# Transposes of the probabilities moved around the scores, and V's matmuls moved ahead of the subtraction of the maxima

## The reference, cut to what matters

```python
x = x + self_attention(layernorm(x))           # 16 heads of 8, a query sees the 32 keys up to itself
x = x + cross_attention(layernorm(x), ctx)     # 16 heads of 8, a window of 16 keys, with biases
x = x + experts(layernorm(x))                  # top 2 of 8, hidden width 512
# each attention: softmax(mask(q @ k.T * scale)) @ v, then @ w_out
```

## Time and profile before

| | us |
|---|---|
| median of 3 runs | 622.54 (619.52 to 624.52) |
| the profiled execution, its own time | 620.3 |
| its span from first to last instruction | 617.9 |
| TensorE busy | 507.6 (82% of the span) |
| VectorE busy | 386.4 (63%) |
| ScalarE busy | 335.4 (54%) |
| GpSimd busy | 311.0 (50%) |

### The profile page before, as it was taken

How to read it: one execution, slowest core, us unless ns; L and a number is a source line. 1 busy time by engine, 2 the same in 40 slices (tenths; PEclk the granted TensorE clock), 3 DMA queues, 4 the chain that set the end, 5 groups by cost and what they waited for, 6 DMA issues and landing times.

```text
span 617.9 us, 30506 instructions
## 1 busy us (share of the span) xinstructions
PE 507.6 (82%) x11885; PEld 413.1 (67%) x11885; DVE 386.4 (63%) x1314; ACT 335.4 (54%) x981; POOL 311.0 (50%) x417
## 2 busy tenths in 40 slices
PE   1769999999988988879788888886179999999940
PEld 1446777777765665657576666655069999999940
DVE  4537788888864567666666666654526666665626
ACT  1547677777776776666666666653223444333410
POOL 3524445444453446655555555654605555545533
PEclk9979999999999999998989899986559999999985
DMA  7160000000000001100000001000222222222229
GB/s 225 54 275 30 22 27 27 28 25 25 27 22 12 16 13 30 34 29 26 26 26 26 26 27 30 28 30 19 76 49 71 70 66 68 70 65 61 56 94 328
DMA packets 36481, 34.92 MB, mean 57 GB/s; under 512 B 5934, under 2 KB 32688, under 8 KB 36161
## 3 DMA queue, kind: packets, MB, share of 16 engines
q1 hardware_dynamic: 20144, 15.42, 7.9%
q10 hardware_dynamic: 11952, 10.07, 5.8%
q0 software_dynamic: 4320, 8.53, 4.1%
HBM read 18.58 MB, written 11.68 MB: 49 GB/s over the span
## 4 chain that ended last, share of the span: by engine, by line
PE 58%; issue 14%; another core or an unknown queue 13%; DVE 4%; DMA 3%; ACT 3%; SPq 2%; ACTq 1%; POOL 1%; DVEq 0%; POOLq 0%
PE p_scores L1006 9%; PE p_probsT L523 7%; PE p_att_bank L513 6%; PE p_scores L408 5%; PE p_att_bank L1015 5%; PE p_v_bank L1015 5%; PE p_scores L453 3%; PE p_scores L401 2%; PE p_v_bank L478 2%; PE p_att_bank L463 2%; PE p_qk L420 2%; PE p_v_bank L494 2%; DVE x L312 1%; PE p_scores L1021 1%
## 5 line engine op out<-in xcount | busy, mean ns | idle before, releaser
L643 POOL TENSOR_TENSOR k_heads<-qk,consts 128x512 f32<-128x512 f32 x64 | 66.7, 1042 | 121.0 <-ACT qk L573 65.7
L1091 POOL DMA_INDIRECT expert_results<-weighted,result_at x71 | 74.7, 1053 | 77.0 <-DVE weighted L1079 41.4
L718 DVE TENSOR_REDUCE shift<-p_scores 128x8 bf16<-128x512 f32 x128 | 82.4, 686 | 34.1 <-PE p_scores L408 33.9
L550 ACT COPY probsT<-p_probsT 128x512 f32<-128x512 f32 x128 | 75.6, 591 | 26.1 <-PE p_probsT L523 24.5
L513 PE MATMUL p_att_bank<-values,probsT 128*32 128x36 f32 x4096 | 66.6, 205 | 24.9 <-issue 24.9
L1055 ACT ACTIVATE hidden<-p_scores 128x512 f32<-128x512 f32 x71 | 42.4, 598 | 77.2 <-PE p_scores L1006 52.2
L523 PE MATMUL p_probsT<-consts,probs 128*128 128x128 f32 x512 | 83.1, 287 | 0.5 <-ACT probsT L550 0.2
L513 PEld LDWEIGHTS p_att_bank<-values,probsT 128*32 128x32 f32 x4096 | 53.3, 111 | 39.6 <-issue 32.9
L556 ACT ACTIVATE probs<-p_scores 128x512 f32<-128x512 f32 x128 | 77.9, 609 | 0.1
L1006 PE MATMUL p_scores<-gotT,w_now 128*128 128x128 f32 x568 | 77.8, 281 | 0.0
L855 POOL DMA_INDIRECT sent_rows<-row,slot_u x64 | 64.3, 1004 | 15.8 <-issue 15.5
(11 more groups left out here) (131 smaller groups left out, 962.6 us busy)
## 6 DMA issues: line engine op xcount, KB each, us to landing
got<-sent_rows ACTq DMA_DIRECT2D x71, 66.0 KB, 1.9
swapped<-raw SPq DMA_DIRECT2D x64, 64.0 KB, 1.9
w<-w_in ACTq DMA_DIRECT2D x2, 2048.0 KB, 11.9
back<-expert_results SPq DMA_DIRECT2D x8, 512.0 KB, 6.8
ctxT<-ctxT_in SPq DMA_DIRECT2D x32, 64.0 KB, 1.9
out<-x SPq DMA_DIRECT2D x8, 256.0 KB, 5.0
x<-x_in SPq DMA_DIRECT2D x4, 448.0 KB, 10.1
expert_results<-weighted,result_at POOLq DMA_INDIRECT x71
```

The costliest lines, as they stand in the source:

```text
L550: nc.scalar.copy(probsT[:, 4 * half:4 * half + 4, :], p_probsT[:, :].rearrange("p (m q) -> p m q", q=P)).then_inc(s_pT, 1)
L643: nc.gpsimd.tensor_tensor(k_heads[:, :, BLK:], qk[:, 1:2, :].to_broadcast([P, G, P]), cv(C_HEAD, G).unsqueeze(2).to_broadcast([P, G, P]), ...
L718: nc.vector.tensor_reduce(shift[:, half * 8:half * 8 + 8], p_scores[:, half * 8:half * 8 + 8, 0:WIN], AX.X, ALU.max).then_inc(s_max, 1)
L1091: nc.gpsimd.indirect_dma_start(out=results, out_offset=bass.IndirectOffsetOnAxis(ap=result_at[:, slot:slot + 1], axis=0), in_=weighted[:, ...
```

## The change

On TensorE `turn_probs(0)` moves to the head of the step, in front of the scores; it waits for the first half of the exponentials alone. `turn_probs(1)` moves right behind the scores. V's matmuls move from behind it to a place between the transpose of the attention output and the subtraction; the transposes of x stay where they were. On ScalarE both copies of the transposed probabilities move to the head of the step, in front of the copies of `p_qk`, and in self-attention the copy to `raw` moves behind both exponentials. No instruction but one wait is added or taken away (V's matmuls of the cross-attention now wait for `s_x3T` themselves).

```diff
 def pe_step(h, c):
+                if runs(h, c, 0):
+                    n = count(0)
+                    nc.tensor.wait_ge(s_probs, 2 * n + 1)
+                    wait(nc.tensor, s_pT, 2 * n)
+                    turn_probs(0).then_inc(s_pTraw, 1)
+                yield
                 if runs(h, c, 1):
                     ...
                         mm.then_inc(s_scores, 1)
                 yield
+                if runs(h, c, 0):
+                    n = count(0)
+                    if not runs(h, c, 1):
+                        nc.tensor.wait_ge(s_probs, 2 * n + 2)
+                    nc.tensor.wait_ge(s_pT, 2 * n + 1)
+                    turn_probs(1).then_inc(s_pTraw, 1)
+                yield
                 ...
                     nc.tensor.transpose(p_attT, att[:, :], ident).then_inc(s_aTraw, 1)
                 yield
-                if runs(h, c, 0):
-                    ...
-                    turn_probs(0).then_inc(s_pTraw, 1)
+                if runs(h, c, 2):
+                    v_bank_read()
+                    if not own and runs(h, c, -3):
+                        nc.tensor.wait_ge(s_x3T, at(-3) + 1)
+                    ...
+                    mm.then_inc(s_vraw, 1)
                 yield
                 (subtraction of the maxima, router, projection)
-                if runs(h, c, 0):
-                    nc.tensor.wait_ge(s_pT, 2 * n + 1)
-                    turn_probs(1).then_inc(s_pTraw, 1)
-                yield
-                if runs(h, c, 2):
-                    v_bank_read()
-                    ...
-                    mm.then_inc(s_vraw, 1)
 def act_step(h, c):
+                if runs(h, c, 0):
+                    copy_probsT(0)
+                yield
+                if runs(h, c, 0):
+                    copy_probsT(1)
+                yield
                 (cross: qk with biases; copy of the transposed output)
-                copy_probsT(0), exponent(0), copy_probsT(1), exponent(1)
+                exponent(0), exponent(1)
+                (self: copy to raw, until now at the head of the step)
```

More of the change, by code:

```diff
@@ L438, in pe_step @@
                 yield
-                if runs(h, c, 0):
[L441 to L444, removed]
-                    turn_probs(0).then_inc(s_pTraw, 1)
+                if runs(h, c, 2):
+                    v_bank_read()
+                    if not own and runs(h, c, -3):
+                        nc.tensor.wait_ge(s_x3T, at(-3) + 1)
+                    src = xnT[:, (c + 2) % 2, :] if own else ctxT[:, (c + 2) % 2, :]
+                    for b in range(NBLK):
+                        pos = b if own else BLOCK_ORDER.index(b)
+                        for g in range(G):
+                            mm = nc.tensor.matmul(p_v[g * BLK:(g + 1) * BLK, b * BLK:(b + 1) * BLK],
+                                                  src[:, pos * BLK:(pos + 1) * BLK], group_cols(wv, g), start=True, stop=True)
+                    mm.then_inc(s_vraw, 1)
                 yield
@@ L464, in pe_step @@
                 yield
-                if runs(h, c, 0):
-                    n = count(0)
-                    nc.tensor.wait_ge(s_pT, 2 * n + 1)
-                    turn_probs(1).then_inc(s_pTraw, 1)
-                yield
-                if runs(h, c, 2):
-                    v_bank_read()
[L474 to L479, removed]
-                    mm.then_inc(s_vraw, 1)
                 if not own and runs(h, c, -2):
@@ L580, in act_step @@
                 yield
-                if runs(h, c, 0):
-                    copy_probsT(0)
-                yield
                 if runs(h, c, 1):
                     exponent(0)
-                yield
-                if runs(h, c, 0):
-                    copy_probsT(1)
                 yield
@@ L593, in act_step @@
                 yield
+                if own and runs(h, c, 3):
+                    n = count(3)
+                    nc.scalar.wait_ge(s_qkraw, n + 1)
+                    wait(nc.scalar, s_qk, n - 1)
+                    nc.scalar.copy(raw[:, (c + 3) % 2, :, :].rearrange("p t k -> p (t k)"), p_qk[:, 0:2 * P]).then_inc(s_raw, 1)
                 if runs(h, c, 3 + ahead):
```

## The result

| | before | after |
|---|---|---|
| median, us | 621.03 (614.23 to 624.52) | 664.8 (660.1 to 670.58) |
| the profiled execution | 620.3 | 663.9 |
| its span | 617.9 | 662.0 |
| mean granted clock | 0.925 | 0.894 |
| TensorE busy | 507.6 (82%) | 518.4 (78%) |

The ratio after to before is 1.072 (95% interval 1.058 to 1.086): slower by 43.8 us in the medians, where 656 (625 to 690) had been forecast. The ratio is taken over the fast executions alone (the 670.58 us of after is left out), so it isn't 664.8 / 621.03.

What follows compares the result with a forecast made beforehand. Self-attention was taken as bound by TensorE's own queue, cross-attention by a ring through GpSimd, TensorE and ScalarE. Self-attention +8, sending steps +19, first cross steps +3, last steps +2 and clock +4 made +36 on 620.3: 656 us, range 625 to 690.

Steps and rivals of the forecast that it cites:

- The ring of self-attention: Self-attention, second turn through ScalarE's queue to the next second turn: 5.32 us, taken as 5.25 against 4.99 a step.
- The wait named on the turn: Self-attention, sign of being right: a named TensorE wait of about 0.6 us for `copy_probsT` in every step.
- the loop's turn: Self-attention, every fourth step: its 0.45 us stall would hide in TensorE's wait for the copy, leaving no difference there.
- `raw` later: Self-attention, ScalarE's copy to `raw` some 3 us later in the step: covered by one step's slack, costed at nothing.
- the +8 us forecast for self-attention: Self-attention: +0.26 us in each of some 30 steps as ScalarE's queue joins the ring; bounds -11 and +13 us.
- The lap of cross-attention: Sending steps, ring through GpSimd, TensorE and ScalarE: 7.31 plus 0.86 for both turns, 8.17 us; 22 steps, +19 us.
- The clock: Sending stretch: 20 us more at 1.2 GHz, a quarter of it lost, +4 us (0 to +30).
- the seven first steps of the cross-attention: Cross-attention before sending begins: half of 0.86 us lost in each step, +3 us (0 to +6).
- the end: The last two or three steps: +2 us.
- A: Rival, cross-attention: transfers hold the transposes of x and ScalarE joins the ring, 1.75 us a step, 675 us; chance 0.24.
- B: Rival, cross-attention: with V ahead of the transfers the stall in probabilities times V goes, 615 us; chance 0.14.
- C: Rival, cross-attention: VectorE or ScalarE bounds it, not the lap; the turns stay hidden, 625 us; chance 0.12.

Runs made afterwards that it cites:

- turns_alone: The changed kernel, but with V's matmuls left behind the projection: 682.2 us against 616.5 for the kernel before, ratio 1.107.
- v_alone: The kernel before, with only V's matmuls moved between transpose and subtraction, in both attentions: 604.9 us against 616.5, ratio 0.982.
- the pair of fillers: The changed kernel and the kernel before, each with eight unused matmuls more per cross-attention step: 639.5 us (ratio 1.037) and 627.2 us (no ratio).
- turns_filler: The changed kernel with V's matmuls left behind the projection, plus eight unused matmuls per cross-attention step: 664.6 us against 620.9 before, ratio 1.072.
- v_cross_sends_late: The kernel before, with V ahead of the subtraction in cross-attention and GpSimd's indirect transfers started later: 622.1 us against 620.9, ratio 1.001.
- sends_late: The kernel before, with GpSimd's two indirect transfers of a step started behind its additions: 609.5 us against 617.5, ratio 0.988.

## Why the prediction was right, and where it was off

**The ring of self-attention** held. Forecast 2.19 + 2.49 + 0.64 = 5.32 and taken as 5.25, measured 1.97 + 2.51 + 0.64 = 5.12. The term that was too long is TensorE's, from the second turn to the first exponential, by 0.10 us before V, 0.07 in V and 0.05 behind it; V's wait is still there (3.2 us in 19 steps on its loads). The wait named on the turn is 0.41 us, not 0.6. The 4.99 that I compared with holds the loop's turn, and I had said that this stall would hide. It didn't: the steps at the turn take 5.49 us, 0.38 more than the others. The two errors nearly cancel: 19 periods grew by 4.1 us where 19 x 0.26 = 4.9 had been said. What I had wrong was the cause in the change: the turns alone don't lengthen the stretch, V's place ahead of the subtraction does (`turns_alone`); and that a path over VectorE's x is as long as the ring.

**A wait not foreseen** stands beside the ring. With the second turn out of the way, L517 comes so early that it waits for VectorE's addition of x (`s_res`):

```profile
PEld p_att_bank L517 <- DVE x L680: 11.8, 19, 0.6
PEld p_probsT L527 <- ACT probsT L554: 7.8, 19, 0.4
```

These are the waits of the 19 self-attention steps (sum, times, longest). They lie on the second path. In the first steps the same wait is long: in step 2 one of 8.8 us, where VectorE stands behind the rotated q and k, and these behind GpSimd's sines, which start at 41.26 us after a pause of 10.3 us that no wait in the profile explains. In before GpSimd had done the sines of that block at 29.83, and it was TensorE that paused, until 40.23, in the next step's masks. I read the +4.6 us ahead of the first window, which the prediction had as part of its 30 equal steps, as this; `raw` later was costed at nothing for the running loop, not for the start. It comes with the turns and ScalarE's order and not with V: the fourth pair of maxima starts at 46.35 us in after and at 46.28 in `turns_alone`, at 41.45 in before and 39.16 in `v_alone`. Which of the two moves on ScalarE brings it, the copies' or `raw`'s, no run separates. So the +8 us forecast for self-attention came about (4.1 + 4.6) by luck: half of it has another cause.

**The lap of cross-attention** held in its path, less in its terms: 8.17 forecast, 7.83 measured in a step at nearly full clock, 8.03 on average with the clock up. In the lap shown the two turns take 0.59 + 0.50 = 1.09 us, not 0.86; the rest of L517 takes 0.41 and not 0.73, since 41 of its 64 matmuls are through before the last stop and not 14; and from the projections to `k_heads` pass 1.39 us and not 1.70. Against before at full clock the order costs 0.61 us a step (up to 0.7, see above), not 0.86, because V, which stood in the lap's shadow by my account, was worth 1.06 us beside the turns (and 0.40 without them, at full clock): costing its move at nothing in cross-attention was wrong, and so was costing the turns at 0.86, which are 1.67 when V stays behind them. The two misses nearly cancel.

**The clock** is the term that was mis-sized: +4 forecast, 13.5 to 16 measured by the pair of fillers. I had taken 20 more microseconds at 1.2 GHz; it was some 35 more. And I had let a quarter of that be lost; it was nearer to half, since in a step at the lower level TensorE's 1.2 us came whole onto the step. The sum came out at 656 against 664.8 since the order was over-priced (19 against 13.5 to 16) and the clock under-priced by 10 to 12. That these two miss in opposite directions is luck too.

**The edges**: the seven first steps of the cross-attention +3.6 (forecast +3), the end +3.2 (+2), the steps between the attentions -0.8.

**The rivals.** A (675) didn't come, for the reason that stood against it: V has moved. B (615) didn't come: L517 stops in every step. C (625) fell with the lap. Of the signs named, two failed: the wait on the turn was 0.41 us and not 0.6, and the loop's turn still made a difference.

## What to carry to other kernels

Cost a move by the rings that it joins, not by its own length: V's 0.46 us of matmuls, moved by a few places, was worth +0.24 us a step in one attention and -0.40 to -1.06 in the other. When a ring closes, look for a second path of the same length before shortening the first. Look for the transfers with which a group of small-tile matmuls will coincide before moving either, since two moves that each helped took back all of it together. And where one engine waits more, read the granted clock of that stretch: it can cost as much again as the order itself, and a few matmuls that nobody reads may give it back.

## What the runs showed of the hardware

- Matmuls with a 128x32 tile (the probabilities') that meet GpSimd's issuing of an indirect transfer stop and go on 0.4 to 0.5 us behind its end, before the transfer's data move (298.70 against 298.87 in before). TensorE runs without a gap while the second transfer's data move.
- What TensorE has issued behind such matmuls, V's too, reaches ScalarE and VectorE late, 0.6 to 1.0 us behind that end: a wait of 3.45 us for `xnT` in `turns_filler`, 2.35 us for the exponentials in `v_cross_sends_late`, both named "remote". Where only 128x128 matmuls stood in front, ScalarE had its result 0.52 us behind the transpose (409.24 in after). V's matmuls show no gap of their own: in the last sending step of `sends_late` V begins at 394.65, the issuing ends at 395.31, and `xnT` starts at 396.05, 0.74 us behind that. Why the tile matters stays open, and no run tries another tile in the same place.
- In such a stretch the recorded starts of matmuls run ahead of their results, so the consumer's start is the one to read.
- The granted clock rose with work that was not needed, in all four pairs: 0.86 to 0.99 with eight 128x256 matmuls a step (and the step became 0.83 us shorter), 0.75 to 0.99, 0.94 to 1.00, and 0.87 to 0.94 with four. V's move alone raised it too, from 0.94 to 0.99, with no matmul more.
